# Two attention layers on one core: output biases as columns, another order of the start, value copies among exponentials

## What is computed

```python
xn = group_norm(x, gamma, beta)          # 32 groups of 8 channels, statistics over an image
q, k, v = xn @ wq + bq, xn @ wk + bk, xn @ wv + bv
attn = softmax(q @ k.T / 16)             # 1024 x 1024 for an image
x = (attn @ v) @ wp + bp + x
```

## Time and profile before

| | us |
|---|---|
| median of 3 executions (lowest to highest) | 259.56 (259.39 to 259.83) |
| the profiled execution, its own time | 259.21 |
| its span, first to last instruction | 257.5 |
| PE busy | 247.9 |
| DVE busy | 186.9 |
| ACT busy | 149.7 |
| POOL busy | 125.1 |

### The profile page before, as it was taken

One profiled execution on the slowest core, in us unless ns is written; L12 is line 12 of the kernel. 1 busy time (PEld: TensorE's weight loads), 2 busy tenths in 40 slices (PEclk: granted clock), 3 DMA queues, 4 the chain that ended last, 5 costly groups with the idle time before them and its releaser, 6 DMA issues.

```text
span 257.5 us, 4562 instructions
## 1 busy us (share of the span) xinstructions
PE 247.9 (96%) x1558; PEld 223.3 (87%) x1558; DVE 186.9 (73%) x489; ACT 149.7 (58%) x291; POOL 125.1 (49%) x151
## 2 busy tenths in 40 slices
PE   8999798999999999999998999999998999999995
PEld 6886678889998899889997899789997899889995
DVE  0588599788995788677956898677866788558904
ACT  3655343499995408940996607940996708830930
POOL 2010800378488506901795925901695936800770
PEclk9999999999999999999999999999999999999999
DMA  6998000000025001320132001320010001100112
GB/s 202 334 187 219 1 0 0 3 1 3 0 83 83 2 0 43 82 41 3 42 82 42 3 0 43 83 41 3 22 62 0 3 0 43 41 0 3 42 41 81
DMA packets 34766, 12.62 MB, mean 49 GB/s; under 512 B 26284, under 2 KB 34488, under 8 KB 34744
## 3 DMA queue, kind: packets, MB, share of 16 engines
q1 hardware_dynamic: 34720, 12.33, 18.9%
q10 hardware_dynamic: 24, 0.01, 0.1%
HBM read 8.14 MB, written 4.19 MB: 48 GB/s over the span
## 4 chain that ended last, share of the span: by engine, by line
PE 69%; DVE 14%; ACT 8%; issue 7%; POOL 1%; ACTq 0%; DVEq 0%; POOLq 0%
PE ring L1101 11%; PE ring L1103 10%; PE ring L1102 10%; PE ring L1075 9%; PE ring L1076 9%; PE ring L1077 9%; ACT P_hi L496 3%; ACT S L497 2%; DVE R L714 2%; PE ring L1048 2%; PE ring L1050 2%; PE ring L1049 2%; DVE xraw L581 2%; DVE bn L586 1%; PE ring L1061 1%
## 5 line engine op out<-in xcount | busy, mean ns | idle before, releaser
L357 POOL TENSOR_TENSOR P_lo<-S,P_hi 128x512 fp32r<-128x512 f32 x64 | 81.8, 1306 | 54.4 <-ACT S L497 54.4
L1101 PE MATMUL ring<-V,P_hi 128*128 128x258 f32 x256 | 72.7, 284 | 0.0
L1103 PE MATMUL ring<-V,P_lo 128*128 128x258 f32 x256 | 72.4, 283 | 0.0
L1102 PE MATMUL ring<-V,P_hi 128*128 128x256 f32 x256 | 72.3, 282 | 0.0
L496 ACT ACTIVATE P_hi<-S 128x512 fp32r<-128x512 f32 x64 | 40.2, 628 | 32.2 <-DVE S L773 32.0
L489 ACT COPY S<-ring 128x512 f32<-128x512 f32 x64 | 36.8, 590 | 33.7 <-PE ring L1077 32.9
L1075 PE MATMUL ring<-t_hi,xn_lo 128*128 128x512 f32 x128 | 50.2, 392 | 1.8 <-DVE out_bias L614 1.5
L1076 PE MATMUL ring<-t_lo,xn_hi 128*128 128x512 f32 x128 | 49.9, 390 | 0.0
L1077 PE MATMUL ring<-t_hi,xn_hi 128*128 128x512 f32 x128 | 49.8, 389 | 0.0
L1101 PEld LDWEIGHTS ring<-V,P_hi 128*128 128x128 f32 x256 | 48.5, 189 | 0.4
L1102 PEld LDWEIGHTS ring<-V,P_hi 128*128 128x128 f32 x256 | 48.3, 189 | 0.4
(11 more groups left out here) (114 smaller groups left out, 355.5 us busy)
## 6 DMA issues: line engine op xcount, KB each, us to landing
xnat<-in_x SPq DMA_DIRECT2D x8, 256.0 KB, 4.0
between<-xnat SPq DMA_DIRECT2D x16, 128.0 KB, 1.8
out<-xnat SPq DMA_DIRECT2D x16, 128.0 KB, 1.7
moved<-in_x SPq DMA_DIRECT2D x8, 128.0 KB, 3.8
moved<-between SPq DMA_DIRECT2D x16, 64.0 KB, 2.3
moved<-between SPq DMA_DIRECT2D x32, 32.0 KB, 2.0
wide<-in_vectors SPq DMA_DIRECT2D x2, 384.0 KB, 7.1
w_wq<-in_L_conv_wq SPq DMA_DIRECT2D x2, 256.0 KB, 4.2
```

The source lines that it names most:

```text
L357: nc.gpsimd.tensor_tensor(P_lo[:, exp_of(c, kb), :], S[:, tile_of(c, kb), :], P_hi[:, exp_of(c, kb), :].bitcast(F32), ALU.subtract).then_i ...
L1101: nc.tensor.matmul(bank[:, 0:C + 2], P_hi[:, tile, mine], v[:, kb, 0:C + 2], start=(kb == 0), stop=False)
L1102: nc.tensor.matmul(bank[:, 0:C], P_hi[:, tile, mine], v[:, kb, C + 2:VX], start=False, stop=False)
L1103: last = nc.tensor.matmul(bank[:, 0:C + 2], P_lo[:, tile, mine], v[:, kb, 0:C + 2], start=False, stop=(kb == NB - 1))
```

## The change

It has these parts:

- **Biases as columns.** `output_bias(l)` on PE makes bv wp as two columns of 128 channels (four float32 matmuls of one column, wp as the stationary operand). DVE adds bp to them from `vec_cols` (`bias_columns`, two instructions of 2 elements), PE turns each of the four columns, broadcast, into 128 equal rows (`output_biases_to_all`, four transposes), DVE copies both layers out at once (`output_biases`). The row `bp` is no longer loaded to all partitions (`WIDE` has two vectors), and only the score tile in the last bank waits for the copy.
- **x transposed in one go.** `A_product(0, 1)` stands behind all four groups of x transposes; the transposes of layer 1's wq and wk, mean and variance of unit 0, and both `Wx_product(0, .)` change places; ACT and DVE follow in their orders. `Wx_low(0, 0)` comes before the first `xn_low`.
- **First t by quarters of x.** `t_product` waits for each 128-channel part of xn_lo only before it uses it. `Wx_product(1, 1)` stands between the two halves of unit 0's t.
- **Statistics of unit 1.** The first `statistics_of(1, 0)` stands ahead of the running maxima, the aggregation behind the fourth maximum, `mean_of_groups(1)` behind value block 0, `variance_of_groups(1)` behind block 3; the ring order follows.
- **Values copied among exponentials.** For units 2 and 3, value blocks 0 to 3 are copied behind exponentials 3, 4, 5 and 6 of the chunk before. In every unit from 1 on, `t_high` of the second half stands one exponential earlier, and `t_low` one `shifted` earlier.

```diff
-WIDE = VECTORS[3:]
+WIDE = VECTORS[3:5]
...
-    ring_order += [("M", 1)]
-    ring_order += [("V", 0, m) for m in range(3)]
+    ring_order += [("V", 0, 0), ("M", 1)]
+    ring_order += [("V", 0, m) for m in range(1, 4)]
     ring_order += [("G", 1)]
...
+        def bias_bank(l):
+            return ring[RING - 1][:, (l + 1) * KC:(l + 2) * KC]
...
-                if r == 1:
+                if r == 2:
                     A_high(0, 0)
...
+            weight_transposed(1, 1)
             Wx_high(0, 0)
             Wx_high(0, 1)
-            weight_transposed(1, 1)
...
-                for m in range(NB):
+                for m in range(0 if u == 1 else 4, NB):
                     v_high(u, m)
-                    if m in (2, 5):
+                    if m == 5 or u == 1 and m == 2:
                         exponentials(before, 6 + m // 3)
...
-                    if kb in (3, 4):
-                        t_high(u, 1, kb - 3)
+                    if kb in (2, 3):
+                        t_high(u, 1, kb - 2)
                     exponentials(first, kb)
...
                     exponentials(second, kb)
+                    if more and kb >= 3:
+                        v_high(u + 1, kb - 3)
+                if more:
+                    exponentials(second, 6)
+                    v_high(u + 1, 3)
...
-            def output_bias(l):
-                dve.wait_ge(ld_wide[l], 16)
+            def bias_columns():
                 dve.wait_ge(pe_ob, LAYERS)
-                nc.vector.tensor_tensor(out_bias[:, l, :], ring[RING - 1][:, l * C:(l + 1) * C], wide[:, l, WIDE.index("bp"), :],
-                                        ALU.add).then_inc(dv_ob, 1)
+                for l in range(LAYERS):
+                    nc.vector.tensor_tensor(bias_col[:, l, :], bias_bank(l), vec_cols[:, :, l * NV + VECTORS.index("bp")],
+                                            ALU.add).then_inc(dv_oc, 1)
+
+            def output_biases():
+                dve.wait_ge(pe_oa, 1)
+                nc.vector.tensor_copy(out_bias[:, :, :], ring[RING - 1][:, :].rearrange("p (l c) -> p l c", l=LAYERS)
+                                      ).then_inc(dv_ob, 1)
...
             normalise(0, range(0, 2))
+            Wx_low(0, 0)
             xn_low(0, 0)
             xn_low(0, 1)
             attention_vector(0, 0)
             attention_vector(0, 1)
             normalise(0, range(2, 4))
-            for k in range(KC):
-                Wx_low(0, k)
+            bias_columns()
+            Wx_low(0, 1)
...
-            for l in range(LAYERS):
-                output_bias(l)
+            output_biases()
             for k in range(KC):
                 Wx_low(1, k)
+            statistics_of(1, 0)
             for kb in range(1, NB):
                 running_max(0, kb)
-                if kb > NR:
-                    attention_vector(1, kb - NR - 1)
-                if kb <= NR:
-                    statistics_of(1, kb - 1)
+                if kb >= NR:
+                    if kb > NR:
+                        attention_vector(1, kb - NR - 1)
+                else:
+                    statistics_of(1, kb)
                 if kb == NR:
                     channel_statistics(1)
...
-                    if u > 1 and m in (1, 4):
-                        shifted(before, 6 + m // 3)
+                    if u > 1 and m == 4:
+                        shifted(before, 7)
...
+                t_low(u, 1, 0)
                 shifted(first, 4)
-                t_low(u, 1, 0)
+                t_low(u, 1, 1)
                 shifted(first, 5)
-                t_low(u, 1, 1)
...
                     t_low(u + 1, 0, 1)
+                    shifted(second, 6)
...
-                for kd in range(KC):
-                    last = nc.tensor.matmul(ring[RING - 1][:, l * C:(l + 1) * C], vec_cols[:, kd, r:r + 1].to_broadcast([P, P]),
-                                            w_raw[l, "wp"][:, kd, :], start=(kd == 0), stop=(kd == KC - 1))
+                for k in range(KC):
+                    for kd in range(KC):
+                        last = nc.tensor.matmul(bias_bank(l)[:, k:k + 1], w_raw[l, "wp"][:, kd, k * P:(k + 1) * P],
+                                                vec_cols[:, kd, r:r + 1], start=(kd == 0), stop=(kd == KC - 1))
                 last.then_inc(pe_ob, 1)
 
+            def output_biases_to_all():
+                pe.wait_ge(dv_oc, LAYERS)
+                for l in range(LAYERS):
+                    for k in range(KC):
+                        last = nc.tensor.transpose(ring[RING - 1][:, l * C + k * P:l * C + (k + 1) * P],
+                                                   bias_col[:, l, k:k + 1].to_broadcast([P, P]), ident[:])
+                last.then_inc(pe_oa, 1)
...
-                        pe.wait_ge(dv_ob, LAYERS)
+                    if ring_place[tile] == RING - 1:
+                        pe.wait_ge(dv_ob, 1)
...
-                if r < KC:
-                    A_product(0, r)
+                if r == 0:
+                    A_product(0, 0)
+            A_product(0, 1)
             transpose_weight(0, 2)
             output_bias(0)
+            mean_of_groups(0)
             transpose_weight(1, 0)
-            mean_of_groups(0)
-            Wx_product(0, 0)
+            transpose_weight(1, 1)
             variance_of_groups(0)
-            Wx_product(0, 1)
-            transpose_weight(1, 1)
+            for mc in range(KC):
+                Wx_product(0, mc)
             transpose_weight(1, 2)
...
-                if k == 0:
-                    wait_for_x_low(pe, u, (h + 1) * KC)
...
+                    if k == 0:
+                        wait_for_x_low(pe, u, h * KC + kc + 1)
...
-            for h in range(HALVES):
-                for k in range(KC):
-                    t_product(0, h, k)
+            for k in range(KC):
+                t_product(0, 0, k)
             Wx_product(1, 1)
+            for k in range(KC):
+                t_product(0, 1, k)
+            output_biases_to_all()
             for kb in range(NB):
                 scores(0, kb)
-            mean_of_groups(1)
             for m in range(NB):
                 values(0, m)
+                if m == 0:
+                    mean_of_groups(1)
                 if m == 2:
                     maxima_by_query(0)
+                if m == 3:
                     variance_of_groups(1)
```

More of the change, by code:

```diff
@@ L76, in two_attention_layers @@
     ring_order += [("S", 0, kb) for kb in range(NB)]
-    ring_order += [("M", 1)]
-    ring_order += [("V", 0, m) for m in range(3)]
+    ring_order += [("V", 0, 0), ("M", 1)]
+    ring_order += [("V", 0, m) for m in range(1, 4)]
     ring_order += [("G", 1)]
-    ring_order += [("V", 0, m) for m in range(3, NB)]
+    ring_order += [("V", 0, m) for m in range(4, NB)]
     ring_order += [("S", 1, kb) for kb in range(NB)]
@@ L124, in two_attention_layers @@
         eps = sb("eps", [P, LAYERS])
+        bias_col = sb("bias_col", [P, LAYERS, KC])
         out_bias = sb("out_bias", [P, LAYERS, C])
@@ L198, in two_attention_layers @@
         pe_ob = sem("pe_ob")
+        pe_oa = sem("pe_oa")
         pe_xT = sem("pe_xT")
@@ L224, in two_attention_layers @@
         dv_Wx = sem("dv_Wx")
+        dv_oc = sem("dv_oc")
         dv_ob = sem("dv_ob")
@@ L942, in output_bias @@
                 pe.wait_ge(ld_w[l, "wp"], 16)
+                if l:
+                    pe.wait_ge(dv_stat, VARE)
                 r = l * NV + VECTORS.index("bv")
-                for kd in range(KC):
-                    last = nc.tensor.matmul(ring[RING - 1][:, l * C:(l + 1) * C], vec_cols[:, kd, r:r + 1].to_broadcast([P, P]),
-                                            w_raw[l, "wp"][:, kd, :], start=(kd == 0), stop=(kd == KC - 1))
+                for k in range(KC):
+                    for kd in range(KC):
+                        last = nc.tensor.matmul(bias_bank(l)[:, k:k + 1], w_raw[l, "wp"][:, kd, k * P:(k + 1) * P],
+                                                vec_cols[:, kd, r:r + 1], start=(kd == 0), stop=(kd == KC - 1))
                 last.then_inc(pe_ob, 1)
+            def output_biases_to_all():
[5 more added lines that the diff above has]
+                last.then_inc(pe_oa, 1)
             def transpose_rows(bank, r):
@@ L1014, in _ @@
                 transpose_rows(ring[2 + r % 2], r)
-                if r < KC:
-                    A_product(0, r)
+                if r == 0:
+                    A_product(0, 0)
+            A_product(0, 1)
             transpose_weight(0, 2)
             output_bias(0)
+            mean_of_groups(0)
             transpose_weight(1, 0)
-            mean_of_groups(0)
-            Wx_product(0, 0)
+            transpose_weight(1, 1)
             variance_of_groups(0)
-            Wx_product(0, 1)
-            transpose_weight(1, 1)
+            for mc in range(KC):
+                Wx_product(0, mc)
             transpose_weight(1, 2)
-            pe.wait_ge(dv_stat, VARE)
             output_bias(1)
```

## The result

The changed kernel takes 253.07 us (median of 6 executions, 252.42 to 254.79) against 259.48 us for the kernel before (6 executions). The ratio is 0.9757, with a 95% interval of 0.9736 to 0.9778. The forecast was 253.2 us in a range of 252.1 to 255.1.

What follows compares the result with a forecast made beforehand. PE, busy 247.9 of 257.5 us, bounds the kernel, so the change must fill its holes. Gains of 6.35 us take the profiled 259.21 to 252.9; the median stands 0.35 above, so 253.2 us, range 252.1 to 255.1.

Steps and rivals of the forecast that it cites:

- all four kinds: PE's named waits, 5.0 us together: on DVE's `out_bias`, the group statistics `mv`, `w_row` (twice) and `t_lo`.
- The head, 10.3 to 18.4: First `output_bias` to first t on PE: one-column products cost as before, 0.16 us of idle won, t at 18.25.
- D: Rival, chance 0.04: PE's clock granted at the lower level (1.2 GHz) from about 10 us on, 261.3 us.
- First scores: PE's first scores start at 25.4 us, not 27.17, 1.8 earlier; `Wx_product(1, 1)` covers the wait for `xn_lo`.
- Shift of chunk 0: PE's shift step comes at 42.36 us, not 45.49, gain 3.1; DVE still last, by 0.3.
- Value copies: Units 2 and 3: PE's whole hole at the eighth value block goes, 1.2 us each.
- t_lo: PE's waits for DVE's `t_lo` go: 0.25 us in unit 1 (104 us), 0.6 at 162.49, slack there about 0.9.
- Quarters of x: First t on PE: waits by quarters gain nothing, since PE comes later than both quarters.
- The sum: Whole kernel: gains of 3.1 + 0.25 + 1.2 + 0.6 + 1.2 = 6.35 us off the profiled execution's 259.21.
- B: Rival, chance 0.15: start gives half, one-column matmuls expose weight loads (1.7 us) or DVE's steps come later; 254.9 us.
- C: Rival, chance 0.10: copies among the exponentials do little, the hole reappears at the scores or `t_lo`; 256.2 us.
- E: Rival, chance 0.05: PE and not DVE ends last in the first stage, 3.6 us in place of 3.1; 252.7 us.

## Why the prediction was right, and where its terms were off

- **The bound.** PE's holes set the time, and all four kinds went. With the parts put back one at a time, their waits came back in their old places.
- **The head, 10.3 to 18.4.** The one-column products cost what the mean's pair said: 0.83 us a layer, 0.10 each, against my 0.11. The fall of the clock (D) did not come in the changed kernel; with 16 x transposes and 24 of weights all slices of its clock row are at the full level. From the first `output_bias` to the first t PE takes 7.69 us in place of 8.14: 0.45 gained where I had 0.16. In the kernel before, four transposes and the wait at the mean take 0.76 (11.24 to 12.00), and four such transposes 0.43 (14.26 to 14.69), so this hole was 0.3 from start to start and not its bracket of 0.16.
- **First scores.** Forecast 25.4, measured 25.06. But the reason needs a change: the experiments with biases as rows show that only the wait's place gains. That was in my sum (the third tile wants `out_bias`, not the first), though it stood under the biases as columns. The forecast also had `Wx_product(1, 1)` cover the wait for `xn_lo`. With that product moved back the wait did not return, so the cover gave nothing; what brought `xn_lo` forward was not tested.
- **Shift of chunk 0.** Forecast 42.36 with DVE last by 0.3, measured 42.09 with DVE last by 0.66. The gain at this point is 3.4 and not 3.1, but from the first t it is 3.03 where the forecast had 2.97 (27.08 less 42.36 - 18.25), so DVE's chain was sized right and the difference lies in the head. PE's own side I had at 42.0, 23.75 from the first t; with DVE lighter it took the shift at 41.46, 23.4 from the first t. That is where the longer wait comes from.
- **Value copies.** Forecast 2.4 for both places, 2.2 by the medians and 2.3 in the trace when undone.
- **t_lo.** 0.25 + 0.6 = 0.85 in the sum, 0.9 when undone. In the expectation for that experiment I let the value copies take 0.3 us of it, which the trace did not bear out; in the sum of the prediction that error could not show, since the parts stood together. There it sits in the slack, forecast at 0.9: the second `t_lo` of unit 2 ends at 156.27 and PE starts that score at 156.93, 0.7 us later.
- **Quarters of x.** Forecast at nothing, and nothing was measured.
- **The sum.** 6.35 from the profiled execution, 6.4 by the medians (259.48 - 253.07), 6.8 between the two profiled executions. The rivals B, C, D and E did not occur. That the sum and the medians meet within 0.1 us is partly luck: the starts of single executions lie further apart than that (last section).

## What to carry to other kernels

Where the busiest engine is at 96%, list its holes from start to start, each with its releaser, and price each edit by the hole that it stands at; the edits then add, as long as the chain that follows has slack. Before rewriting how a thing is made, ask who really needs it first: here one wait moved two tiles on gave 1.7 us, and the rewritten product gave nothing. When a hole of the bound engine closes, the engine next in line (here DVE, by 0.66 us) is where the next gain lies, and work with a late use, such as the attention vectors, is the first to move out of its chain.

## What the runs showed of the hardware

**Idle time may cost twice.** In one execution of the kernel with biases as before, with a wait of 2.32 us in front of the scores, the granted clock fell to 0.50 for some 3.4 us, 1.3 us after PE had taken up work again, and cost about 1.6 us more. Of the five executions of this kernel only this one fell clearly (mean clock 0.993, the others 0.998 to 1.0). The kernel before has a wait of 1.46 us at the same place, and its profiled execution keeps the full clock. The Trainium skill ("TensorE: Matmul & The Clock Gate", Part 1) has the clock fall back when the engine has been idle. The trace of that one execution agrees, with the fall some time after the work had begun again. That the wait was the cause is not shown: the other four executions ran the same program, wait included by all that is known of them, and kept the clock.

**The start differs from execution to execution.** The first t began at 18.04 us in the changed kernel and at 19.54 in the kernel with the quarters undone, whose head is the same. The DMAs of x explain part of it. This is from PE's timeline of the second:

```profile
9.21 1.41 PE L985 MATMUL ring<-ident,xnat 128*128 128x128 f32 x8 [0.70 <-DMA xnat<-in_x]
...
19.54 0.58 PE L1081 MATMUL ring<-xn_hi,A_lo 128*128 128x512 f32 x1
```

Its slowest part of x took 6.3 us from issue to landing, in the changed kernel 5.0, in the kernel before 4.9. But the landing is not all. In the kernel with the old order of the head PE never waited for x, and its first t still began at 18.91. There the weight loads waited 0.3 us each for the weights `w_wv` and `w_wp` to land, and PE's steps at the start were longer:

```profile
5.17 1.11 PE L939 MATMUL ring<-ident,w_wk 128*128 128x128 f32 x4
6.08 0.89 PE L985 MATMUL ring<-ident,xnat 128*128 128x128 f32 x4
```

From start to start these four transposes of wk took 0.91 us without a wait between them, the same four in the kernel before 0.61 (5.16 to 5.77), and four later ones 0.43 (14.26 to 14.69). In the kernel before, too, the very first four took 1.02 (3.84 to 4.86). The profile's granted clock is 1.00 in all these stretches, so what makes the first steps long stays open; the prediction had read the clock row alone and taken the first transposes as running at full pace.

So executions with the same head differ by up to 1.5 us at the first t, and the order of the head could not be judged by whole times. What can be compared is the part behind the first `output_bias`: it takes 7.69 us in the changed kernel and 7.75 with the old order (11.16 to 18.91), where this time there was no wait at the mean. The order by itself is worth under 0.1 us there. Whether it saves the wait at the mean, 0.3 us in the kernel before, and what it does ahead of 10.3 us, stays open.
